# Attention in turns of 32 queries by 4 heads, with the next heads' projections beside each turn

## The reference

```python
x = x + xattn(layernorm(x), ctx, bias, Wq, Wk, Wv, Wo)      # x (4, 128, 512), ctx (4, 2048, 512)
q = split_heads(query @ Wq, 16) * 32 ** -0.5
k = split_heads(ctx @ Wk, 16)
v = split_heads(ctx @ Wv, 16)
logits = einsum('bhqd,bhkd->bhqk', q, k) + bias             # bias (1, 1, 128, 2048)
weights = softmax(logits, axis=-1)
out = einsum('bhqk,bhkd->bhqd', weights, v) @ Wo
```

## Time and profile before

| | |
|---|---|
| median of 3 runs | 1005.3 us |
| profiled execution, first to last instruction | 1003.4 us |
| around that span (median less span) | 1.9 us |
| PE busy | 970.8 us (97%) |
| DVE, ACT, POOL busy | 599.4, 488.4, 258.3 us |
| up to the first product with Wo (line 542) | 624.8 us |
| from there to the end | 378.6 us |

### The profile page before, as it was taken

The page is one execution under the profiler, slowest core; times in us unless marked ns, Lnnn a source line. Parts: engine busy times, 40 slices in busy tenths (PEclk is TensorE's granted clock), DMA queues, the critical chain, the costliest instruction groups (busy, mean ns, idle before and its releaser), DMA issues. The chain is left out here.

```text
span 1003.4 us, 18226 instructions
## 1 busy us (share of the span) xinstructions
PE 970.8 (97%) x7342; PEld 815.7 (81%) x7350; DVE 599.4 (60%) x1178; ACT 488.4 (49%) x633; POOL 258.3 (26%) x254
## 2 busy tenths in 40 slices
PE   9999999999999999999999999987899999999996
PEld 8888788888778888788888787554589999999995
DVE  6517895565886467886364886685652112455552
ACT  4211885171886155787051687578621102455551
POOL 2202830002840001850000760678400201111100
PEclk9999999999999999999999999999999999999999
DMA  8294861524771615781421787400079949699930
GB/s 293 71 192 85 179 153 46 212 84 120 176 171 49 275 42 168 173 199 46 164 83 48 173 177 267 157 2 0 33 270 382 373 165 332 227 381 345 336 110 13
DMA packets 77597, 169.92 MB, mean 169 GB/s; under 512 B 6473, under 2 KB 17609, under 8 KB 72385
## 3 DMA queue, kind: packets, MB, share of 16 engines
q1 hardware_dynamic: 75392, 163.87, 53.2%
q0 software_dynamic: 2112, 4.80, 2.1%
HBM read 119.01 MB, written 16.10 MB: 135 GB/s over the span
## 5 line engine op out<-in xcount | busy, mean ns | idle before, releaser
L995 POOL CAST stack<-kT 128x2048 fp32r<-128x2048 f32 x32 | 62.8, 1976 | 381.4 <-ACT kT L850 374.0
L712 DVE CUSTOM_DVE_ANT_0 prob<-psum,biasmap,top 128x512 f32<-128x512 f32 x192 | 144.2, 751 | 15.5 <-PE psum L482 7.0
L894 ACT ACTIVATE prob<-prob,top 128x2048 f32<-128x2048 f32 x64 | 128.7, 2010 | 37.7 <-DVE top L712 37.7
L2319 PE MATMUL psum<-xT,wring 128*128 128x128 f32 (+3 forms) x1024 | 133.9, 291 | 0.4 <-ACT xT L2673 0.4
L502 PE MATMUL psum<-ident,prob 128*128 128x128 f32 x1024 | 130.8, 274 | 1.3 <-ACT probT L902 1.3
L2319 PEld LDWEIGHTS psum<-xT,wring 128*128 128x128 f32 x1024 | 130.4, 191 | 1.8 <-ACT xT L2673 0.7
L502 PEld LDWEIGHTS psum<-ident,prob 128*128 128x128 f32 x1024 | 116.7, 140 | 16.0 <-issue 4.4
L850 ACT COPY kT<-psum 128x512 f32<-128x512 f32 x64 | 37.5, 585 | 188.9 <-PE psum L414 188.7
L429 PE MATMUL psum<-wv_hi,ctx_part 128*128 128x512 f32 x256 | 99.9, 390 | 0.1
L431 PE MATMUL psum<-wv_hi,ctx_part 128*128 128x512 f32 x256 | 99.7, 389 | 0.0
L430 PE MATMUL psum<-wv_lo,ctx_part 128*128 128x512 f32 x256 | 99.6, 389 | 0.0
(11 more groups left out here) (284 smaller groups left out, 1771.0 us busy)
## 6 DMA issues: line engine op xcount, KB each, us to landing
wring<-in_w SPq DMA_DIRECT2D x64, 1024.0 KB, 8.6
ctx_raw<-in_ctx_t SPq DMA_DIRECT2D x15, 1024.0 KB, 6.0
stack<-stack SPq DMA_DIRECT2D x32, 256.0 KB, 4.7
early_stack<-early_stack SPq DMA_DIRECT2D x28, 256.0 KB, 3.8
prob<-in_w_gate_t SPq DMA_DIRECT2D x1, 5632.0 KB, 17.5
stack<-key_stack SPq DMA_DIRECT2D x20, 256.0 KB, 4.0
query_stacks<-prob SPq DMA_DIRECT2D x16, 256.0 KB, 5.4
qstack<-query_stacks SPq DMA_DIRECT2D x16, 256.0 KB, 5.2
```

Of the source, the lines that this page charges most:

```text
L712: dve.tensor_tensor_reduce(prob[:, slot, keys], psum[:, scores.of[n, j, c], :], biasmap[:, keys], 1.0, top[:, h, (c + 1) % 2:(c + 1) % 2 + ...
L894: act.activation(prob[:, slot, :], prob[:, slot, :], ACT.Exp, bias=top[:, h, 1:2], scale=-1.0, accum_out=top[:, h, 2:3]).then_inc(*raised. ...
L2319: mm = pe.matmul(psum[:, w, 0:width], wring[piece][:, k, h % 4 * P:(h % 4 + 1) * P], xT[:, q % 2, k, 0:width], start=(k == 0), stop=(k == ...
```

## The change

The attention is cut into 64 turns. A turn `s` is one quad of heads by one block of 32 queries (quad `s // 4`, block `s % 4`).

- **Scores in 32x32 tiles.** The stacked keys, their splits and their DMAs go. `score` issues 16 plain float32 matmuls of 512 columns with 32 rows and 32 output partitions each: head `j` picks the row group and the PSUM bank, key range `a_` the column group. Partitions then hold key ranges by queries, so the minimum over keys needs one more step: `turn_top` (a transpose), `join_ranges` (DVE), `spread_least` (four small matmuls), and a copy of it at the head of `raise_turn`, which then takes four exponentials of 512.
- **Turning by VectorE.** `transpose_turn` turns 128x2048 probabilities in 32x32 blocks from SBUF to SBUF. The 1024 transposes on PE and the 96 copies of 1024 out of PSUM go. `multiply_quad` issues the same products as before, all of a quad at once, in the turn with `s % 4 == 1` behind the quad; `fold_sums` brings the softmax sums across the key ranges.
- **Projections beside the turns.** Keys and values of two quads (256 columns) are projected per pass over a batch's context: a list of 64 visits of one chunk each, so each chunk is loaded and split four times, twice for keys and twice for values. Visits 0 to 3 come before turn 0; the other 60 are spread over turns 0 to 59, as parts (quarters of a visit), 5, 2, 4 and 5 in the four turns of a quad. The last four turns have none. ACT makes the high part (`high_of_ctx`), POOL the low part (`low_of_ctx`) from visit 4 on; both follow the end of the visit two before, since there are two buffers.
- **Ternary weights in 26 pieces of 1024,** one per turn: DVE sums piece `s` in turns 0 to 25 (`sum_weights`), the means come in turn 26, and in turns 27 to 52 DVE scales a piece, POOL clips it (`clip_weights`) and ACT casts it one turn later (`make_ternary`).
- The tail of the last batch in the next layer is shorter: `spread_least` of the last turn, then the products with Wo with `multiply_quad` of the last quad between them.

```diff
+PARTS_OF_VISIT = 4
+PARTS = (5, 2, 4, 5)
+VISITS = [("keys", 0, c) for c in range(CHUNKS)]
+for h_ in range(STAGES):
+    VISITS += [("values", h_, c) for c in range(CHUNKS)]
+    if h_ + 1 < STAGES:
+        VISITS += [("keys", h_ + 1, c) for c in range(CHUNKS)]
...
+SUM_FIRST = 0
+MEAN_AT = SUM_FIRST + len(TERNARY)
+SCALE_FIRST = MEAN_AT + 1
...
             project_first_keys()
-            for b in range(B):
...
+            for r in range(PARTS_OF_VISIT):
+                project_part(1, r)
+            turn_x()
+            project_queries()
+            for i in (2, 3):
+                for r in range(PARTS_OF_VISIT):
+                    project_part(i, r)
+            for s in turns:
+                score(s)
+                if s:
+                    spread_least(s - 1)
+                n = quad_weighed_in(s)
+                if n is not None:
+                    multiply_quad(n)
+                    fold_sums(n)
+                parts = parts_of(s)
+                for i, r in parts[:-1]:
+                    project_part(i, r)
+                if s == MEAN_AT:
+                    join_sums()
+                turn_top(s)
+                for i, r in parts[-1:]:
+                    project_part(i, r)
...
+            def add_bias(s, j):
...
+                dve.wait_ge(*scored.at(s, j))
                 dve.tensor_tensor_reduce(
...
+            def transpose_turn(s):
+                n, block = divmod(s, BLOCKS)
+                dve.wait_ge(*raised.at(s))
+                if block == 0 and n:
+                    dve.wait_ge(*multiplied.at(n - 1))
+                dve.transpose(probT[:, :, block, :],
+                              places_of(s).rearrange("p j (k r) -> p (j k) r", r=DH)).then_inc(*transposed.made(s))
...
+            def join_ranges(s):
+                dve.wait_ge(*top_turned.at(s))
...
+            for s in turns:
+                for j in range(QUAD):
+                    add_bias(s, j)
+                if s:
+                    transpose_turn(s - 1)
+                join_ranges(s)
...
+                if step_in(s, SUM_FIRST) is not None:
+                    sum_weights(step_in(s, SUM_FIRST))
...
+                if step_in(s, SCALE_FIRST) is not None:
+                    scale_weights(step_in(s, SCALE_FIRST))
...
+            def high_of_ctx(i):
+                act.wait_ge(*ctx_in[i % 2].at(i))
+                if i >= 2:
+                    act.wait_ge(*visit_done(i - 2))
+                act.copy(ctx_part[:, i % 2, 0, :, :], ctx_raw[:, i % 2, :, :]).then_inc(*ctx_high.made(i))
...
+            def copy_unit(i, r):
+                kind, h, c = VISITS[i]
+                if r % 2:
+                    (copy_keys if kind == "keys" else copy_values)(h, c, r // 2)
+                if r == PARTS_OF_VISIT - 1 and i + 2 < len(VISITS):
+                    high_of_ctx(i + 2)
...
+            def raise_turn(s):
+                n, block = divmod(s, BLOCKS)
+                act.wait_ge(*least_spread.at(s))
+                act.copy(shift[:, s % 2, :], least_out).then_inc(*shifted.made(s))
+                act.wait_ge(*shifted.at(s))
+                for j in range(QUAD):
+                    exp = act.activation(places_of(s)[:, j, :], places_of(s)[:, j, :], ACT.Exp,
...
+            for s in turns:
+                if s:
+                    raise_turn(s - 1)
+                if step_in(s, SCALE_FIRST + 1) is not None:
+                    make_ternary(step_in(s, SCALE_FIRST + 1))
+                for i, r in parts_of(s):
+                    copy_unit(i, r)
...
+            def low_of_ctx(i):
+                pool.wait_ge(*ctx_high.at(i))
...
+            def clip_weights(p):
+                place = piece_place(len(TERNARY) + p)
+                pool.wait_ge(*scaled.at(p))
...
+            low_of_ctx(4)
+            low_of_ctx(5)
+            for s in turns:
+                if step_in(s, SCALE_FIRST) is not None:
+                    clip_weights(step_in(s, SCALE_FIRST))
+                for i, r in parts_of(s):
+                    if r == PARTS_OF_VISIT - 1 and i + 2 < len(VISITS):
+                        low_of_ctx(i + 2)
...
+            def load_ctx(i):
+                kind, h, c = VISITS[i]
+                if i == 2:
+                    sp.wait_ge(*slice_low.at("ctx", DT - 1))
+                elif i > 2:
+                    sp.wait_ge(*ctx_low(i - 2))
```

More of the change, by code:

```diff
@@ new lines, in ctx_low, with visit_done, parts_of @@
+        def ctx_low(i):
+            return (ctx_low_v if i < CHUNKS else ctx_low_g).at(i)
+        def visit_done(i):
+            kind, h, c = VISITS[i]
+            return (keys_projected if kind == "keys" else values_projected).at(h, c, 1)
+        def parts_of(s):
+            first = sum(PARTS) * (s // BLOCKS) + sum(PARTS[:s % BLOCKS])
+            parts = [divmod(CHUNKS * PARTS_OF_VISIT + p, PARTS_OF_VISIT) for p in range(first, first + PARTS[s % BLOCKS])]
+            return [(i, r) for i, r in parts if i < len(VISITS)]
@@ L432, in project_value_tile @@
[L432 to L440 removed]
+                w, columns = work.of["values", h, c, pair], slice((h % 2) * HALF, (h % 2 + 1) * HALF)
@@ new lines, in project_values @@
+                place = psum[:, w, at * HALF:(at + 1) * HALF]
+                keys_of = lambda part, k: ctx_part[:, i % 2, part, k, kk * P:(kk + 1) * P]
+                for k in range(DT):
+                    if (h, c, kk) == (0, 0, 0):
+                        pe.wait_ge(*slice_low.at("wv", k))
+                    pe.matmul(place, keys_of(0, k), wv_hi[:, k, columns], start=(k == 0), stop=False)
+                    pe.matmul(place, keys_of(0, k), wv_lo[:, k, columns], start=False, stop=False)
+                    mm = pe.matmul(place, keys_of(1, k), wv_hi[:, k, columns], start=False, stop=(k == DT - 1))
@@ new lines, in fold_sums, with join_sums @@
+            def fold_sums(n):
+                for block in range(BLOCKS):
+                    for j in range(QUAD):
+                        mm = pe.matmul(sums_out[j * DH:(j + 1) * DH, block * DH:(block + 1) * DH],
+                                       sums[:, n % 2, block, j:j + 1].broadcast_to([P, DH]), fold[:, :], start=True,
+                                       stop=True, tile_position=(0, j * DH))
+                mm.then_inc(*sums_folded.made(n))
+            def join_sums():
+                pe.wait_ge(*weights_summed.at(len(TERNARY) - 1))
+                pe.wait_ge(*shifted.at(MEAN_AT - 1))
+                pe.matmul(mean_out, ones[:, :], wsum[:, :], start=True, stop=True).then_inc(*sums_joined.made("all"))
@@ L765, in ternary_step, with find_means @@
+            def find_means():
+                dve.wait_ge(*sums_joined.at("all"))
+                first = 0
+                for mats in (MATS[0:4], MATS[4:5], MATS[5:6]):
+                    those = slice(MATS.index(mats[0]), MATS.index(mats[-1]) + 1)
+                    count = sum(piece[0] in mats for piece in TERNARY)
                     dve.tensor_reduce(wmean[:, 0, those],
-                                      mean_out[:, 0:len(window.sums)].rearrange("p (m s) -> p m s", m=count), AX.X,
@@ L948, in scalar_attention @@
-            return raise_head, move_pair
+                act.copy(wk_hi[:, k, :], wk_sb[:, k, :]).then_inc(*slice_high.made("wk", k))
+            high_of_ctx(1)
+            act.wait_ge(*wq_in.at("all"))
+            act.copy(wq_hi[:, :, :], wq_sb[:, :, :]).then_inc(*slice_high.made("wq"))
+            for r in range(PARTS_OF_VISIT):
+                copy_unit(0, r)
+            for r in range(PARTS_OF_VISIT):
+                copy_unit(1, r)
+            copy_rows()
+            act.wait_ge(*wv_in.at("all"))
```

1128 lines of the change are left out of this document (362 added, 766 removed).

## The result

| | before | after |
|---|---|---|
| median, same chip | 1005.2 us | 1109.3 us (1109.16 to 1109.68, 4 runs) |
| ratio | | 1.1035, 95% 1.1019 to 1.1051 |
| profiled span | 1003.4 us | 1107.6 us |
| PE busy | 97% | 85% |

The kernel became 10.3% slower. The prediction was 1077.0 us, range 990 to 1150.

The account below looks back on a forecast made before the run. PE alone was taken to bound the part before the first product with Wo (busy 617.9 of 624.8 us). 56 + 489.4 + 2 + 95 + 22 + 27 + 3 + 380.6 gave 1075 us span, 1077 median; range 990 to 1150.

Parts of the forecast that it names:

- 1040 to 1110: Whole kernel: the branch in which the stalls come as worked out, time 1040 to 1110 us, chance 0.50.
- rival of 1108: VectorE's turning costs twice, 4.6 us: 31 us more, 1108; turning or drains toward 1110 and over, together 0.07.
- rival of 1096: PE drains at each tile shape change: +2.5 x 15, half absorbed in stalls, 1096; turning or drains together 0.07.
- turn 0 starts: Start: four visits and the queries, waiting for loads and splits, put turn 0 at 56 us.
- sixty turns, unstalled: Turns 0 to 59 on PE: 32.9 us per quad, 15 x 32.9 - 4.1 = 489.4 us.
- stalls for `ctx_part`: PE waiting for POOL's low parts: 9 x 2.2 + 6 x 5.7 = 54, 7 of 5.8 us, 41; together 95.
- slow clock in the turns: PE at half speed after thirteen stalls: 1.7 us each, between nothing and 2.3, 22 us.
- last four turns: Turns without projection parts: 27 us to the last turn's `spread_least`, plus 3 for the slow clock.
- from the first product with Wo: Rest of the program: 378.6 + 2, 380.6 us; 20 us to the first projection where 18.4 passed before.
- rivals of 1127 and 1167: Score tiles overlap across row groups only by pairs, 1127, or not at all, 1167; scores beyond 1110, chance 0.13.
- A clip 2.7 (half of 5.41): POOL's clip of a piece in turns 27 to 52, ahead of the low part: 2.7 us.
- The faster rival: Context parts ready in time: 957 us without any stall, 990 with the short stall alone; chance 0.17.

Follow-up runs that it names:

- run 3: Kernel after, with context high and low parts made in halves, each with its own event, clip still ahead on POOL: 1065.3 us, 1.0605 of the kernel before.
- run 1: Kernel after, with the clip behind the low parts in POOL's queue instead of ahead: 1075.4 us, 1.0687 of the kernel before.
- run 2: Kernel after, with the clip moved from POOL to VectorE, right behind the scaling: 1041.2 us, 1.0336 of the kernel before.
- Run 4: Kernel after, with 22 filler matmuls of 128x128 on PE ahead of each of the thirteen long waits: 1089.1 us, 1.0836 of the kernel before.
- run 7: As run 6, and at the start VectorE makes chunk 1's low part ahead of the layernorm: 1020.0 us, 1.0157 of the kernel before.
- run 9: As run 6, with each turn's context load ahead of the ternary pieces' store and load on SP: 1025.6 us, 1.0209 of the kernel before.
- run 10: As run 8, with each turn's context load ahead of the ternary pieces' store and load on SP: 1093.1 us, 1.0880 of the kernel before.
- run 8: Kernel after, with clip on VectorE and high and low parts in halves, `make_ternary` in its old place: 995.2 us, 0.9894 of the kernel before.
- run 5: As run 2, and `make_ternary` behind the copies of its turn on ACT: 1051.8 us, 1.0447 of the kernel before.
- run 6: As run 5, with the high and low parts in halves as in run 3: 1014.9 us, 1.0087 of the kernel before.

## Why the prediction was right, and where it was off

The direction and the mechanism were right: the stalls at `ctx_part`, above all in the scaling stage, through POOL's clip. Its sum was 1075 us of span, 1107.6 came; the time lies at the upper edge of its likeliest branch, "1040 to 1110". By the number alone the rivals of 1108 and 1096 fit better, but the trace shows neither mechanism (below).

| term | predicted | measured |
|---|---|---|
| turn 0 starts | 56 | 55.6 |
| sixty turns, unstalled | 489.4 | 502.8 (by difference) |
| `find_means` | 2 | 3.8 |
| stalls for `ctx_part` | 95 | 95.0 |
| slow clock in the turns | 22 | 31 (worked out below) |
| last four turns | 30 | 30.4 |
| from the first product with Wo | 380.6 | 389.0 |

- **PE's own work.** The score tiles: 32 records start within 0.55 us and the last ends 1.14 us after the first began. "I take 1.0, as the nearest row shows tiles at full overlap" held (0.88 us pass to the next product), and the rivals of 1127 and 1167 fall. The turns of a quad with key parts take 8.4, 8.8, 7.1 and 8.4 us where no stall is left (run 3), 32.7 in sum, those with value parts 8.8, 8.9, 7.3 and 8.8, 33.8; predicted was 32.9 for both. That is some 6 of the 13 us; PE's wait for `shift`, 0.5 us in each of the turns with `s % 4 == 1`, is in it, and the sum did not name it. About as much again is what a stall costs beside its listed idle time, which begins only when the last matmul's latency is over: the turns 3, 7, 11, 15, 19 and 23 are 1.5 to 1.9 us longer than in run 3, where the listed idle time is 1.25 to 1.61, so 0.25 to 0.3 more each, an estimate of 6 us for 22 stalls. Some turns with `s % 4 == 1` take 9.1 to 9.9 instead of 8.9; one holds a pause of 0.91 us at 176.02, in which PE waited for nothing that the profile shows. As the slow clock's 31 us are an estimate, these parts are no exact account.
- **The change of tile shape.** The timeline of PE, a projection and the scores behind it:

```profile
339.37 0.40 PE L305 MATMUL psum<-ctx_part,wk_lo 128*128 128x512 f32 x1
339.70 1.14 PE L400 MATMUL psum<-keys_and_values,q_all 32*32 32x512 f32 x32
```

The scores start 0.33 us later where the pace is 0.23: 0.1, as taken; nothing here supports the rival of 1096. By the drain rule of the Trainium skill (TensorEngine Tiling (Array Packing), Tiling Modes) it would be up to a latency, 0.27 to 0.45; the trace does not bear that out as a cost here.

- **VectorE's turning** is 2.31 us in the mean of 64 rows, 2.30 to 2.32 (predicted 2.3, where no row was shown). The rival of 1108 falls. The Trainium skill (Vector Engine (DVE) Microarchitecture Reference, section 3.8) has one element per cycle and lane, from which the estimate was 2.1 us plus a fixed part: the trace agrees.
- **The stalls.** 95 us is right as a sum and not by its parts; that it agrees to 0.1 us is luck. Of the nine short ones eight are 1.25 to 1.62 us, not 2.2, and the ninth, in turn 27, does not show, since PE waits for the means there; the 22nd wait is one of 0.64 us in turn 0, which was not forecast. The thirteen long ones are 5.7 to 6.7 (82.6 in all), not 5.7 and 5.8. Two steps of the chain were mis-sized, and in opposite directions.
- **The clip's length.** "A clip 2.7 (half of 5.41)" takes 3.63; the row was one multiplication and the clip applies two operations, but no run shows that this makes the difference. Runs 1 and 2 show the cause of the long stalls: the clip's place in the queue, then its engine.
- **The exponentials' length.** They are listed with 0.711 + 0.187 us, more than the 0.624 + 0.188 of the row with bf16 output, and yet four of them take 2.9 us and not the 3.25 of "4 x (0.624 + 0.188)", since the rows overlap: one exponential starts 0.70 us behind the other:

```profile
107.92 0.72 ACT L693 ACTIVATE prob<-prob,shift 128x512 f32<-128x512 f32 x1
108.56 0.19 ACT L693 ACTIVATION_READ_ACCUMULATOR prob<-prob,shift 128x1 f32 x1
108.65 0.71 ACT L693 ACTIVATE prob<-prob,shift 128x512 f32<-128x512 f32 x1
```

So ACT is done earlier than predicted (in turn 6, the turn of these rows, the last exponential ends 4.5 us into the turn, where 4.85 was taken), which is a part of why the short stalls are shorter. A sum of listed lengths is too long where rows overlap; DVE's additions, summed as 0.685 + 0.083, start 0.61 us apart.

- **The slow clock.** "I let each cost 1.7 us" was too little. In turns 27 to 53 PE's busy time at half clock is 62.2 us, of which half, 31, is an estimate of the cost. Run 4, which took nearly all of it away, gained 20 with its fillers' cost inside. So 20 to 31, 1.6 to 2.4 per stall: the term's upper end was the nearer one. That end, 2.3, was read from the program's start, where the earlier trace rows has the granted clock at 1.00, so its row does not show the lower level.
- **The tail.** "380.6" misses 8.4 us. From the first product with Wo to the first ternary projection pass 27.5 us (18.4 before, 20 predicted); the rest is 361.6 against 360.2. The last four turns leave PE idle for one to three microseconds at a time, and the clock is at its lower level for the 17 us from 707.6 on, so the first 16 records with Wo take 10.17 us, where eight took 3.60 before. In those 27.5 us some 10 of PE's work are at the lower level, by half of it an estimate of 5 of the 7.5 us that 20 was short; PE's wait of 2.5 us for POOL's `spread` is there too. The prediction gave the slow clock 3 us ahead of that point and nothing behind it. In runs 4, 7, 9 and 10 the part from the first product with Wo took 385 us. There 11.0 to 14.2 us of PE's work in it are at the lower level, 19.4 in the kernel after, which by half is about 3 of the 4 us; why the clock differs is open.
- **The start.** 56 was right in the kernel after, 55.6; in the runs with the same start turn 0 begins at 57.3 to 59.5, so the hit to 0.4 us is luck.
- **The faster rival** was priced at 990 for the short stalls alone, and 957 without any. "It wins if [...] the clip takes about 1 us or less": on VectorE, run 2, it does (1.11 us in the mean, 0.69 when alone) and the kernel was still at 1041. With halves as well, run 8 reached 995. What kept it from 957 are, among others, the longer turns (the 6 us above), the tail (388.3 instead of 380.6), waits for `ctx_part` (5.1), pauses of PE (9.0, below) and the start (turn 0 at 58.3).

That the new order wins at all, by 1%, needed two edits; run 8 is the version to use. The kernel before has no waits of this kind on PE, so the two edits would not carry to it; that was not tried.

## What to carry to other kernels

When work is spread beside other work, sum each engine's time, but price the order: take each buffer's release and follow the chain of queues to its next reader, engine by engine and SP's queue too. A filler job (here a clip of 3.6 us) ahead of the late link costs its whole length at every boundary (behind the low part, run 1, the thirteen waits were 3.8 us shorter in the mean), and moving it sets the next queue's order: runs 5 and 9 each shortened one wait and lengthened another, and run 10 only lost. Where a part can't start earlier, let its reader start on half of it.

## What the runs showed of the hardware

**VectorE held up by GpSimd.** In the turn of `find_means` a tensor_scalar on four columns took 4.28 us, where the same operation on one column took 0.15 just behind it. It ended with POOL's subtraction beside it, which ran from 292.47 to 296.98. VectorE's timeline of the kernel after:

```profile
292.73 4.28 DVE L587 TENSOR_SCALAR wmean<-wmean 128x4 f32<-128x4 f32 x1
...
297.11 0.15 DVE L587 TENSOR_SCALAR wmean<-wmean 128x1 f32<-128x1 f32 x1
```

The 3.8 us that PE waited for the means are this. In run 8 the clip on VectorE takes 2.27 us in the mean of 21, where one with POOL idle takes 0.69 (run 6, at 376.14), and in one case 2.75 from 372.27 on, beside a half subtraction of POOL's from 372.09 to 374.47 and the next, which follows at once. In run 2 two of the 26 take 5.0 and 5.1 us. The Trainium skill (SBUF — State Buffer, Who interferes with whom) says that such an operation of VectorE's can contend with GpSimd for a port pair that they share, and that the one that issues first holds it for its whole instruction while the other is blocked; the trace agrees in the first case, to 0.1 us.

**PE pauses inside a row of small tiled matmuls.** In run 8 PE stood 2.48 us in the middle of a quad's products, waiting for nothing that the profile shows; three such pauses at that line come to 5.3 us and three at the folded sums to 3.7, and runs 2 and 9 have them at the products too (4.7 and 5.6). VectorE's turning, released by those products, was late by as much. What causes them is open.
